# Output projection of an attention: the result held tile by tile, turned in place, rings of four in place of gather copies

## The reference

```python
x = x + _L0_attn_ref(_layernorm(x, axis=-1), L0_attn_W_attn, L0_attn_b_attn, L0_attn_W_proj, L0_attn_b_proj)
...
attn = jnp.einsum('bhqk,bhkd->bhqd', probs, v)
attn = attn.transpose(0, 2, 1, 3).reshape(B, S, E)
out = attn @ W_proj + b_proj
...
x = x + _L0_ffn_ref(_layernorm(x, axis=-1), ...)
```

## Time and profile before

| | |
|---|---|
| time, median of 3 runs | 1362.17 us (1360.82 to 1364.11) |
| profiled execution: its own time | 1361.62 us |
| profiled execution: span | 1359.6 us |
| TensorE busy | 1229.7 us (90%) |
| VectorE busy | 862.5 us (63%) |
| ScalarE busy | 571.0 us (42%) |
| GpSimd busy | 248.2 us (18%) |
| mean granted clock of TensorE, share of full speed | 0.954 |
| the block of `project_attention`, from the end of line 681 to the end of the last line 63 | 583.4 to 608.8 us |

### The profile page before, as it was taken

One profiled execution on the slowest core, in us unless ns is written; L12 is line 12 of the kernel. 1 busy time (PEld: TensorE's weight loads), 2 busy tenths in 40 slices (PEclk: granted clock), 3 DMA queues, 4 the chain that ended last, 5 costly groups with the idle time before them and its releaser, 6 DMA issues. The chain is left out here.

```text
span 1359.6 us, 32622 instructions
## 1 busy us (share of the span) xinstructions
PE 1229.7 (90%) x13048; PEld 714.2 (53%) x13080; DVE 862.5 (63%) x1742; ACT 571.0 (42%) x854; POOL 248.2 (18%) x444
## 2 busy tenths in 40 slices
PE   5769999999999999878999968995999999969998
PEld 2433333333333333254677644442888888857775
DVE  6367878888888888345433364897576666643432
ACT  2314777777777776823133214652211111112221
POOL 4220010000001001040277500233222111000000
PEclk9867999999999999998999988997999999979999
DMA  4310112211111220051143320000200000000000
GB/s 127 54 23 4 29 28 40 41 28 27 28 27 29 40 39 3 3 160 62 32 162 101 119 79 0 0 0 5 76 4 4 4 4 3 4 2 0 16 16 31
DMA packets 33836, 49.47 MB, mean 36 GB/s; under 512 B 11995, under 2 KB 22331, under 8 KB 32955
## 3 DMA queue, kind: packets, MB, share of 16 engines
q1 hardware_dynamic: 29211, 36.55, 12.1%
q0 software_dynamic: 3744, 10.23, 2.4%
q10 hardware_dynamic: 768, 1.05, 0.2%
HBM read 23.63 MB, written 9.31 MB: 24 GB/s over the span
## 5 line engine op out<-in xcount | busy, mean ns | idle before, releaser
L664 DVE TENSOR_REDUCE at_block_max<-at_p_ring 128x4 f32<-128x512 f32 x576 | 367.7, 686 | 76.3 <-PE at_p_ring L570 42.2
L641 ACT ACTIVATE at_probs<-at_p_score,abias 128x1024 f32<-128x1024 f32 (+2 forms) x320 | 318.8, 1029 | 123.2 <-PE at_p_score L600 69.0
L570 PE MATMUL at_p_ring<-kt,qt 64*128 64x128 bf16 (+3 forms) x1152 | 187.2, 284 | 18.5 <-PEq L727 7.4
L615 PE MATMUL at_p_out<-at_probs,at_vs 128*32 128x512 f32 (+3 forms) x1536 | 164.5, 500 | 0.4 <-ACT at_probs L641 0.4
L594 PE MATMUL at_p_score<-qt,kt 64*128 64x512 bf16 (+3 forms) x768 | 146.2, 332 | 5.7 <-ACT at_probs L641 4.8
L570 PEld LDWEIGHTS at_p_ring<-kt,qt 64*128 64x128 bf16 x1152 | 69.9, 95 | 130.4 <-DVE at_block_max L664 86.6
L707 POOL TENSOR_TENSOR at_shift<-shift,at_row_max 128x16 f32<-128x16 f32 x32 | 7.1, 221 | 423.2 <-DVE at_row_max L670 423.2
L594 PEld LDWEIGHTS at_p_score<-qt,kt 64*128 64x128 bf16 x768 | 38.4, 94 | 85.7 <-ACT at_probs L641 55.2
L2055 ACT COPY rc_ta<-rc_bank 128x256 f32<-128x256 f32 x32 | 10.3, 375 | 148.9 <-PE rc_bank L1826 148.9
L2184 PE MATMUL fi_p_in<-fi_xt,w_in 128*128 128x512 f32 x128 | 64.2, 626 | 0.7 <-ACT fi_xt L2221 0.7
L600 PE MATMUL at_p_score<-anticausal,ident 128*128 128x128 bf16 (+1 forms) x384 | 62.3, 244 | 0.0
(11 more groups left out here) (334 smaller groups left out, 2153.9 us busy)
## 6 DMA issues: line engine op xcount, KB each, us to landing
qt<-qparts SPq DMA_DIRECT2D x96, 64.0 KB, 2.4
kt<-kparts SPq DMA_DIRECT2D x96, 64.0 KB, 2.5
rows<-moe_chosen SPq DMA_DIRECT2D x4, 1024.0 KB, 4.8
w_routed<-in_w_routed_dram SPq DMA_DIRECT2D x1, 2816.0 KB
x<-in_x_dram SPq DMA_DIRECT2D x4, 512.0 KB, 8.4
moe_table<-rows SPq DMA_DIRECT2D x4, 512.0 KB, 2.7
out_dram<-x SPq DMA_DIRECT2D x4, 512.0 KB, 2.9
w_down<-in_w_down_dram SPq DMA_DIRECT2D x1, 1408.0 KB
```

The source lines that it names most:

```text
L570: mm = pe.matmul(bank[:, col:col + nb * P], qt[nxt][h * ROWS:(h + 1) * ROWS, pair, t * P:(t + 1) * P], kt[nxt][h * ROWS:(h + 1) * ROWS, pa ...
L615: mm = pe.matmul(p_out[32 * h:32 * h + 32, left(k):QC], vs[(now - e[2]) % BUFS][:, key, h, :], probs[g % PROBS][:, h % 2, at:at + w], star ...
L641: act.activation(probs[g % PROBS][:, :, 0:len(pairs) * w], p_score[g % 2][:, :, 0:len(pairs) * w], ACT.Exp, bias=abias[:, c * TPB + key:c ...
L664: dve.tensor_reduce(dst, src, AX.X, ALU.max).then_inc(s["fill_used"], 1)
```

## The change

`attn` changes its order to [128, 8 tiles, 16 units, 32 features]. The 256 features of a token tile and a sequence now lie in one piece, so TensorE turns them where they are; the gather copies on GpSimd and the buffers `tile` are gone. In exchange VectorE's store (line 681) writes four pieces of 32 elements, 512 elements apart, where it was one piece of 128. `turned`, `p_turn` and `p_proj` are rings of four, used in turn by all 16 tiles, which are now taken in their order 0 to 15 (sequence 0 first) and not in pairs. TensorE turns two tiles ahead of the one that it projects. VectorE adds tile j and then takes the statistics of tile j - 1. GpSimd's bias additions wait for nothing.

```diff
--- before.py
+++ after.py
@@ -679,7 +679,7 @@
                     unit = u - e[2]
                     dve.wait_ge(s["dve_chain"], unit * NQC + e[1] + 1)
                     dve.tensor_tensor(
-                        attn[:, ds(unit, 1), 4 * e[1]:4 * e[1] + 4, :].rearrange("p u t (h r) -> p (u t) h r", r=HD),
+                        attn[:, 4 * e[1]:4 * e[1] + 4, ds(unit, 1), :].rearrange("p t u (h r) -> p (t u) h r", r=HD),
                         view[:, :, :, 0:HD], rden[e[1]][:, :, :].unsqueeze(3).to_broadcast([P, QC // P, GROUP, HD]),
                         ALU.mult).then_inc(s["fill_used"], 1)
 
@@ -763,15 +763,16 @@
         sb = lambda n, s, d=F32: ctx.enter_context(nc.sbuf_tensor("pa_" + n, s, d))
         ps = lambda n, s, d=F32: ctx.enter_context(nc.psum_tensor("pa_" + n, s, d))
         sem = lambda n: ctx.enter_context(nc.semaphore("pa_" + n))
-        tile = [sb(f"tile{b}", [P, E]) for b in range(B)]
-        turned = [sb(f"turned{b}", [P, EH, P]) for b in range(B)]
-        p_turn = [ps(f"p_turn{b}", [P, 512]) for b in range(B)]
-        p_proj = [ps(f"p_proj{b}", [P, 512]) for b in range(B)]
-        tile_ready, turn_psum, turn_ready, proj_ready, proj_used, biased = (
-            sem(n) for n in ("tile_ready", "turn_psum", "turn_ready", "proj_ready", "proj_used", "biased"))
-
-        def x_tile(t, b):
-            return x[:, ds(t + b * TPB, 1), :].rearrange("p a e -> p (a e)")
+        RINGED = 4
+        turned = [sb(f"turned{i}", [P, EH, P]) for i in range(RINGED)]
+        p_turn = [ps(f"p_turn{i}", [P, 512]) for i in range(RINGED)]
+        p_proj = [ps(f"p_proj{i}", [P, 512]) for i in range(RINGED)]
+        turn_psum, turn_ready, proj_ready, proj_used, biased = (
+            sem(n) for n in ("turn_psum", "turn_ready", "proj_ready", "proj_used", "biased"))
+        in_group = P // (GROUP * HD)
+
+        def x_tile(j):
+            return x[:, j, :]
 
         with nc.Block() as block:
             @block.sync
@@ -781,54 +782,61 @@
 
             @block.gpsimd
             def _(pool):
-
-                pool.sem_inc(turn_psum, B)
-                pool.sem_inc(proj_used, B)
-                for t in range(TPB):
-                    for b in range(B):
-
-                        pool.wait_ge(turn_psum, t * B + b + 1)
-                        pool.tensor_copy(tile[b][:, :].rearrange("p (g c) -> p g c", g=GPB),
-                                         attn[:, b * GPB:(b + 1) * GPB, ds(t, 1), :].rearrange("p g t c -> p (g t) c")
-                                         ).then_inc(tile_ready, 1)
-                        pool.tensor_tensor(x_tile(t, b), x_tile(t, b), bias[:, :], ALU.add).then_inc(biased, 1)
+                for j in range(TILES):
+                    pool.tensor_tensor(x_tile(j), x_tile(j), bias[:, :], ALU.add).then_inc(biased, 1)
 
             @block.tensor
             def _(pe):
-                for t in range(TPB):
-                    for b in range(B):
-                        pe.wait_ge(tile_ready, t * B + b + 1)
-                        for h in range(EH):
-                            mm = pe.transpose(p_turn[b][:, h * P:(h + 1) * P], tile[b][:, h * P:(h + 1) * P], ident[:, :])
-                        mm.then_inc(turn_psum, 1)
-                    for b in range(B):
-                        pe.wait_ge(turn_ready, t * B + b + 1)
-                        pe.wait_ge(proj_used, t * B + b + 1)
-                        for h in range(EH):
-                            mm = pe.matmul(p_proj[b][:, 0:E], turned[b][:, h, :], w[:, h, :],
-                                           start=h == 0, stop=h == EH - 1)
-                        mm.then_inc(proj_ready, 1)
+                def turn(j):
+                    if j >= RINGED:
+                        pe.wait_ge(turn_ready, j - RINGED + 1)
+                    for h in range(EH):
+                        first = (j // TPB) * GPB + h * in_group
+                        mm = pe.transpose(p_turn[j % RINGED][:, h * P:(h + 1) * P],
+                                          attn[:, j % TPB, first:first + in_group, :].rearrange("p g c -> p (g c)"), ident[:, :])
+                    mm.then_inc(turn_psum, 1)
+
+                def project(j):
+                    pe.wait_ge(turn_ready, j + 1)
+                    if j >= RINGED:
+                        pe.wait_ge(proj_used, j - RINGED + 1)
+                    for h in range(EH):
+                        mm = pe.matmul(p_proj[j % RINGED][:, 0:E], turned[j % RINGED][:, h, :], w[:, h, :],
+                                       start=h == 0, stop=h == EH - 1)
+                    mm.then_inc(proj_ready, 1)
+
+                turn(0)
+                turn(1)
+                for j in range(TILES):
+                    if j + 2 < TILES:
+                        turn(j + 2)
+                    project(j)
 
             @block.scalar
             def _(act):
-                for t in range(TPB):
-                    for b in range(B):
-                        act.wait_ge(turn_psum, t * B + b + 1 + B)
-                        act.copy(turned[b][:, :, :], p_turn[b][:, 0:E].rearrange("p (h c) -> p h c", h=EH)
-                                 ).then_inc(turn_ready, 1)
+                for j in range(TILES):
+                    act.wait_ge(turn_psum, j + 1)
+                    if j >= RINGED:
+                        act.wait_ge(proj_ready, j - RINGED + 1)
+                    act.copy(turned[j % RINGED][:, :, :], p_turn[j % RINGED][:, 0:E].rearrange("p (h c) -> p h c", h=EH)
+                             ).then_inc(turn_ready, 1)
 
             @block.vector
             def _(dve):
-                for t in range(TPB):
-                    for b in range(B):
-                        dve.wait_ge(proj_ready, t * B + b + 1)
-                        dve.wait_ge(biased, t * B + b + 1)
-                        dve.tensor_tensor(x_tile(t, b), p_proj[b][:, 0:E], x_tile(t, b), ALU.add
-                                          ).then_inc(proj_used, 1)
-                    for b in range(B):
-
-                        dve.wait_ge(proj_used, t * B + (B + b + 1))
-                        tile_stats(dve, stats, x, t + b * TPB)
+                def add(j):
+                    dve.wait_ge(proj_ready, j + 1)
+                    dve.wait_ge(biased, j + 1)
+                    dve.tensor_tensor(x_tile(j), p_proj[j % RINGED][:, 0:E], x_tile(j), ALU.add).then_inc(proj_used, 1)
+
+                def statistics(j):
+                    dve.wait_ge(proj_used, j + 1)
+                    tile_stats(dve, stats, x, j)
+
+                add(0)
+                for j in range(1, TILES):
+                    add(j)
+                    statistics(j - 1)
+                statistics(TILES - 1)
 
 
 def normalise_and_turn(nc, tag, x, mean, rstd, ident, xt):
@@ -2350,7 +2358,7 @@
             sb("chunk_masks", [P, 2 * L]), sb("level_masks", [P, len(LEVELS), L]), sb("level1_t", [P, L]), sb("eye", [P, L]))
         with ExitStack() as block0:
             sb0 = sb_in(block0)
-            attn = sb0("attn", [P, UNITS, TPB, GROUP * HD])
+            attn = sb0("attn", [P, TPB, UNITS, GROUP * HD])
             w_proj, b_proj = sb0("w_proj", [P, EH, E]), sb0("b_proj", [P, E])
             w_router, priority = sb0("w_router", [P, EH, EXPERTS]), sb0("priority", [P, EXPERTS])
             route, before, ones = sb0("route", [P, ROUTE_WIDTH]), sb0("before", [P, P]), sb0("ones", [P, P])
```

## The result

The changed kernel takes 1352.31 us in the median of six executions, the kernel before 1361.49 us in the same set: a ratio of 0.9935, 95% interval 0.9915 to 0.9954. Two later sets gave 0.9940 (0.9926 to 0.9954) and 0.9936 (0.9922 to 0.9949). The medians of the three sets differ by 9.2, 7.3 and 8.0 us, so the change gains some 8 us. I had forecast 4.5 us, and a range that ended at 1354.9: the direction was right, the size little more than half of what came.

The account below looks back on a forecast made before the run. TensorE's wait for ScalarE's copy was taken to bound the output projection. From 584.64, projections 13.76, turns 2.9 and clock 1.7 end it at 603.2 instead of 607.68: gain 4.5 us, forecast 1357.4, range 1354.9 to 1360.6.

Parts of the forecast that it names:

- the tile's cost: Output projection on TensorE: four matmuls at 0.86 us plus two turns at 0.23, so 1.09 us a tile.
- the opening: Start of the output projection: without gather copies TensorE turns its first tile at 583.75 instead of 584.34.
- the first projection: Output projection: after three turns and ScalarE's copy, projection 0 starts at about 584.64; before, 585.85.
- the tail: End of the output projection: last two statistics still follow the last sum, 0.42 and 0.74 us, overlapping as before.
- The bound for turns paced by their weight load: Output projection: at 141 ns instead of 0.11 us, 26 turns cost 0.8 us more and the gain is 3.7.
- The block's clock: Output projection: TensorE at half clock for 3.4 us, charged at 1.7 us in the changed block.
- Who comes after: Stages behind the output projection: they move 4.5 us forward; shifted clock falls give about 1 us either way.
- B: Before the first turn: idle 0.93 us instead of 1.52, clock doesn't fall; gain 6.2 us, 1355.4; chance 0.2.
- C: Output projection: turns don't overlap with matmuls, 4.2 us more, gain 0.3, 1361.3; chance 0.17 with gains later stages return.
- D: Attention's store in pieces: 32 stores doubled cost 9.3 us, 4.8 us slower, 1366.4; chance 0.08 with similar unseen losses.

## Why the prediction was wrong in size

**The block: right.** The mechanism (TensorE waits for ScalarE's copy of the same pair), the tile's cost (1.09 forecast, 1.08 measured), the opening (0.59 us earlier forecast, 0.58 measured from line 681 on), the first projection, GpSimd out of the way (done at 595.1, forecast 595.5), line 681 at 291 ns, the tail: each came within 0.1 us or so, but for GpSimd, which was 0.4 us early. The forecast of 4.5 us stands against 4.4 in the two traces on record. The bound for turns paced by their weight load was not needed.

**The block's clock: mis-sized.** I took 3.4 us at half speed from one trace and let it cancel. Over three traces of either kernel the block gained 4.9 us; in one of those of before the fall lasted 6.8 us, and without that trace it is 4.6. While the clock is low, the kernel before still has its waits for copies and for the second gather; the changed kernel keeps TensorE full and had a fall of 3.4 us each time. That the second causes the first is my reading, not shown.

**The step that failed** is "Who comes after", in the words "Where the clock falls and returns there may move by a slice or two, about 1 us either way". I treated the later falls as chance that cancels, and looked at the next block's alone, so the stages behind the block stood in the sum with nothing. The runs show a difference there that doesn't cancel: in the traces the experts are 1.4 us shorter and the rest 0.7, and the clock of all executions says that TensorE spends some 7 us less at 1.2 GHz. A useless delay of 3.9 us takes all of it away again, so it hangs on when the later stages run, and not on the new code. One of these falls, near 674 us, is missing in all three traces of the changed kernel. In the traces 7.2 us of the gain are accounted for: 4.9, 1.4, 0.7 and 0.1. The medians say 7.3 to 9.2, with intervals from 6.3 to 11.6 in the first set; the difference is within what the executions scatter.

**The rivals.** B (the shorter wait before the first turn keeps the clock up) fell: 0.95 us instead of 1.52, and the fall came in all three traces. Filling it to 0.30 us did prevent it, in all three traces with that filling. C (turns that don't overlap with matmuls) fell: two turns take 0.22 us from start to start beside matmuls, each being 273 ns long. The Trainium skill, "TensorE: Matmul & The Clock Gate", section "Part 4: PE-mode transpose", has about 275 ns for one turn in context; the trace agrees with it as a duration. By my estimate from the page's figure, a sum that used it as the price of each of 26 turns would have been some 4 us off. D (the store in pieces) fell: the layout alone measures 0.9996.

**What stays open.** Which shift takes a fall away I can't derive from these rows. By length of the block, the fall near 674 us is missing at 21.4, 23.2, 27.0 and 27.9 us, and there at 21.7, 22.5, 25.1, 25.5 and 26.0. The kernel before has it in two traces and not in the third, at the same place of the wait. So what is shown is that the amount of falls behind the block changes with a delay; that the position of a single wait decides is not shown.

The same page of the Trainium skill, in its section "HAM oscillation — how this bites in real kernels", describes bursts of matmuls that each begin at half clock because of the wait ahead of them. The traces agree in part. Filling a wait took the fall behind it away, and the waits, 1.32 and 0.95 us, are far shorter than the 3 to 5 us of the section's example. But the fall came up to 1.9 us after the wait had ended, and a wait of 1.32 us had none behind it in all three traces of the changed kernel; here the measurements decide.

## What to carry to other kernels

When TensorE turns a tile and then needs the copy of that same tile, put the next tiles' turns between them: two tiles ahead and rings of four took the wait away from the second tile on, and this, not the removed gather copies, was the gain. Check whether the stages behind a change contain short waits of TensorE with a fall of the clock behind them; a shift of the stages can add or take away such falls. In one and the same kernel, the one before, the experts took 202.3 and 203.0 us with the fall near 674 and 201.4 without it. So a gain that is larger or smaller than the changed stage says little until the later stages are compared too. A control with useless work that restores the old length tells such a shift from a real gain.

## What was not expected of the hardware

- Useless matmuls made a kernel faster: 3 to 4 us of 1361, by filling one wait of 1.32 us.
- Useless instructions of VectorE that hold it for 3.9 us made the changed kernel 7.6 us slower.
- The clock fell 1.2 us or less after TensorE had waited only 0.95 us, and not when 0.30 us were left of that wait.
- Writing 128 elements as four pieces of 32, 512 elements apart, takes VectorE 291 ns, the same as in one piece.
